# The FP4 feed-forward stage: magnitudes on ScalarE, products read from PSUM by VectorE, and the norm taken block by block

## The reference, cut to what matters

```python
def fp4_quant_dequant(x):
    xb = x.reshape(shape[:-1] + (shape[-1] // 16, 16))
    scale = jnp.maximum(jnp.max(jnp.abs(xb), axis=-1, keepdims=True) / 6.0, 1e-12)
    xn = xb / scale
    idx = jnp.searchsorted([0.25, 0.75, 1.25, 1.75, 2.5, 3.5, 5.0], jnp.abs(xn))
    return ([0.0, 0.5, 1.0, 1.5, 2.0, 3.0, 4.0, 6.0][idx] * jnp.sign(xn) * scale).reshape(shape)

def fp4_linear(x, w):
    return jnp.einsum('bsk,nk->bsn', fp4_quant_dequant(x), fp4_quant_dequant(w))

def _L2_ffn_ref(x, w_gate, w_up, w_down):            # 128 -> 352 -> 128
    h = jax.nn.silu(fp4_linear(x, w_gate)) * fp4_linear(x, w_up)
    return fp4_linear(h, w_down)

x = x + _L2_ffn_ref(_layernorm(x), w_gate, w_up, w_down)   # layernorm eps 1e-5, no gain or bias
```

## Time and profile before

| | us |
|---|---|
| median of 3 runs | 6759.97 |
| the profiled execution, its own time | 6756.28 |
| its span | 6754.2 |
| the stage of the change within the span | 5973 to 6452.7 |

### The profile page before, as it was taken

One profiled execution on the slowest core, in us unless ns is written; L12 is line 12 of the kernel. 1 busy time (PEld: TensorE's weight loads), 2 busy tenths in 40 slices (PEclk: granted clock), 3 DMA queues, 4 the chain that ended last, 5 costly groups with the idle time before them and its releaser, 6 DMA issues. The chain is left out here.

```text
span 6754.2 us, 122147 instructions
## 1 busy us (share of the span) xinstructions
PE 5795.9 (86%) x38509; PEld 3594.7 (53%) x38509; DVE 4329.9 (64%) x9722; ACT 2805.1 (42%) x4568; POOL 1939.8 (29%) x2617
## 2 busy tenths in 40 slices
PE   8996999999993998889987998799888889845567
PEld 5773444444442776467745775477545556523454
DVE  6874666666655775367736774477545466669965
ACT  4552222222221554345543554355444455412244
POOL 5440000000003553255414552355310022333312
PEclk9998999999996999899998999899988899867789
DMA  4332222233223553155504551355300000000002
GB/s 129 104 101 91 96 96 95 96 96 97 95 93 82 144 149 94 31 143 146 138 4 131 149 150 33 88 145 149 80 4 0 3 0 0 4 3 0 0 2 57
DMA packets 526309, 526.84 MB, mean 78 GB/s; under 512 B 55698, under 2 KB 436705, under 8 KB 503780
## 3 DMA queue, kind: packets, MB, share of 16 engines
q1 hardware_dynamic: 526004, 523.15, 27.6%
HBM read 337.88 MB, written 185.07 MB: 77 GB/s over the span
## 5 line engine op out<-in xcount | busy, mean ns | idle before, releaser
L362 DVE TENSOR_REDUCE a_mx<-a_unit 128x2 f32<-128x512 f32 (+1 forms) x1920 | 1294.3, 684 | 574.8 <-PE a_unit L538 562.6
L452 ACT ACTIVATE a_prob<-a_slot 128x1536 f32<-128x1536 f32 x640 | 929.0, 1452 | 740.9 <-PE a_slot L561 448.5
L536 PE MATMUL a_unit<-a_sk,a_sq 96*128 96x256 bf16 (+3 forms) x5120 | 756.3, 251 | 75.2 <-DMA a_sk<-a_kscratch 54.1
L1148 ACT ACTIVATE f_silu<-f_pG 128x512 f32<-128x512 f32 x528 | 315.1, 598 | 939.3 <-PE f_pG L1221 939.1
L1094 DVE TENSOR_TENSOR f_gated<-f_spread,f_silu 128x512 f32<-128x512 f32 x512 | 354.3, 692 | 402.8 <-ACT f_silu L1148 358.3
L538 PE MATMUL a_unit<-a_maskq,identb 128*128 128x256 bf16 (+1 forms) x1920 | 606.3, 316 | 0.0
L1200 PE MATMUL f_pO<-f_hidden,f_wd 128*128 128x512 f32 x1056 | 546.3, 599 | 17.0 <-DVE f_hidden L1096 16.3
L536 PEld LDWEIGHTS a_unit<-a_sk,a_sq 96*128 96x128 bf16 (+1 forms) x5120 | 385.3, 99 | 312.1 <-issue 124.8
L1221 PE MATMUL f_pG<-f_xnT,f_wg 128*128 128x512 f32 x1056 | 541.5, 594 | 0.0
L1225 PE MATMUL f_pU<-f_xnT,f_wu 128*128 128x512 f32 x1056 | 540.9, 594 | 0.0
L60 POOL TENSOR_SCALAR f_veps<-f_moments 128x4 f32<-128x4 f32 (+1 forms) x112 | 25.4, 227 | 1731.3 <-DVE f_moments L1002 1271.4
(11 more groups left out here) (394 smaller groups left out, 11507.0 us busy)
## 6 DMA issues: line engine op xcount, KB each, us to landing
f_spread<-f_scratch SPq DMA_DIRECT2D x1024, 128.0 KB, 2.9
a_sq<-a_qscratch SPq DMA_DIRECT2D x128, 768.0 KB, 5.7
a_sk<-a_kscratch SPq DMA_DIRECT2D x160, 384.0 KB, 6.6
a_qscratch<-a_parts SPq DMA_DIRECT2D x288, 192.0 KB, 2.2
a_qscratch<-a_parts SPq DMA_DIRECT2D x288, 128.0 KB, 2.2
a_kscratch<-a_parts SPq DMA_DIRECT2D x160, 192.0 KB, 2.2
a_kscratch<-a_parts SPq DMA_DIRECT2D x160, 128.0 KB, 2.1
a_qscratch<-a_parts SPq DMA_DIRECT2D x288, 64.0 KB, 1.8
```

The lines of the kernel that those rows point to most:

```text
L362: v.tensor_reduce(dst, src, op=ALU.max, axis=AX.X, negate=True).then_inc(red_done, 1)
L452: act.activation(prob[gr % 2][:, :], slot[:, :], ACT.Exp, scale=SCALE).then_inc(exp_done, 1)
L536: pe.matmul(bank[:, at * wide:(at + 1) * wide], q, sk[b][0:KM, gr * GH + h, 0:wide], start=(at == 0), stop=False)
L1148: act.activation(silu[c % 2][:, :], pG[c % 2][:, :], ACT.Silu).then_inc(silu_done, 1)
```

## The change

`fp4_feed_forward` is rewritten; no other stage is touched.

- `row_moments` is no longer called. VectorE takes `bn_stats` and `bn_aggr` of block n+2 in `step(n)`, GpSimd makes `rstd` and `shift = -mean * rstd` for its four tiles (four instructions of 128x4), and ScalarE writes `xn = x * rstd + shift`, one activation per tile.
- SyncE no longer waits before the loads; GpSimd zeroes only the 32 unused partitions of two slices of `raw`.
- The quantiser is in three parts. `scaled` (five instructions) gives the signed `y = x / scale`; ScalarE writes `|y| * (2^22+1)` (`absx`, `absh`); `rounded` is two scalar_tensor_tensor on the signed numbers, `y = max(mag, c) + y`, then `y = max(mag, c) - y`, which leaves the rounded number with its sign turned; `unscaled` multiplies by a scale that is kept negative.
- The copies `up` are gone. VectorE multiplies `pU` in PSUM with `silu`; `product(0)` of block m stands between `rounded` and `unscaled` of block n, products 1 to 3 behind `unscaled`. `hid` has one buffer.
- TensorE's matmuls of tile t >= 2 wait for the product of tile t-2 (`hid_done`), where they waited for its SiLU.
- All engines step from n = -2; the weights are quantised at the end of that step.

```diff
-    row_moments(nc, core, tag + "m_", core["x"], 1e-5)
...
-        centred = k.sb("centred", [P, BT, D])
+        stats = k.sb("stats", [P, BT, 6]); moments = k.sb("moments", [P, BT, 2]); mhalf = k.sb("mhalf", [P, BT])
+        veps = k.sb("veps", [P, BT]); rstd = k.sb("rstd", [P, BT]); away = k.sb("away", [P, BT]); shift = k.sb("shift", [P, BT])
         xn = k.sb("xn", [P, BT, D]); xq = k.sb("xq", [P, BT, D]); xqT = k.sb("xqT", [P, BLK])
-        amax = k.sb("amax", [P, WIDE // B16]); scl = k.sb("scl", [P, WIDE // B16]); inv = k.sb("inv", [P, WIDE // B16])
-        mag = k.sb("mag", [P, WIDE]); low = k.sb("low", [P, WIDE]); high = k.sb("high", [P, WIDE])
+        amax = k.sb("amax", [P, WIDE // B16])
+        nscx = k.sb("nscx", [P, BLK // B16]); nsch = k.sb("nsch", [P, WIDE // B16]); inv = k.sb("inv", [P, WIDE // B16])
+        yx = k.sb("yx", [P, BLK]); yh = k.sb("yh", [P, WIDE]); absx = k.sb("absx", [P, BLK]); absh = k.sb("absh", [P, WIDE])
         silu = [k.sb(f"silu{b}", [P, I]) for b in range(2)]
-        up = [k.sb(f"up{b}", [P, I]) for b in range(2)]
-        hid = [k.sb(f"hid{b}", [P, BT, I]) for b in range(2)]; hq = k.sb("hq", [P, BT, I])
+        hid = k.sb("hid", [P, BT, I]); hq = k.sb("hq", [P, BT, I])
         hT = [k.sb(f"hT{b}", [P, 3 * P]) for b in range(2)]
...
+        by16 = lambda x: x.rearrange("p (b e) -> p b e", e=B16)
...
-                sp.wait_ge(setup, 1)
...
-                g.memset(raw[:, :, :], 0.0).then_inc(setup, 1)
-
...
+                chain = Chain(g)
+                chain.link(g.memset(mhalf[:, :], -0.5))
+                for c in (2, 5):
+                    g.memset(raw[I - 2 * P:P, c, :], 0.0).then_inc(setup, 1)
+                    g.drain()
+
+                def step(i, j):
+                    n = i * 2 + j
+                    if is_block(n + 2):
+                        g.wait_ge(stats_done, n + 3)
+                        if is_block(n + 1):
+                            g.wait_ge(xn_done, n + 2)
                         g.sem_inc(apart, 1)
...
+                        chain.link(g.tensor_scalar_add(veps[:, :], moments[:, :, 1], 1e-5))
+                        g.tensor_scalar(away[:, :], moments[:, :, 0], -1.0, None, ALU.mult)
+                        chain.link(g.tensor_tensor(rstd[:, :], veps[:, :], mhalf[:, :], op=ALU.pow))
+                        g.tensor_tensor(shift[:, :], away[:, :], rstd[:, :], op=ALU.mult).then_inc(rstd_done, 1)
+                blocks_by_two(g, step)
 
...
-                def quantise(src, dst, width):
+                link = chain.link
+                def scaled(src, dst, nsc, width):
                     nb = width // B16
...
+                    link(v.tensor_reduce(amax[:, 0:nb], by16(src), op=ALU.max, axis=AX.X, apply_absolute_value=True))
+                    link(v.tensor_scalar(nsc, amax[:, 0:nb], -1.0 / 6.0, -1e-12, ALU.mult, ALU.min))
+                    link(v.tensor_scalar(inv[:, 0:nb], nsc, -HALF_DOWN, None, ALU.mult))
+                    link(v.reciprocal(inv[:, 0:nb], inv[:, 0:nb]))
+                    return v.tensor_tensor(by16(dst), by16(src), inv[:, 0:nb].unsqueeze(2).broadcast_to((P, nb, B16)),
+                                           op=ALU.mult)
+                def rounded(y, magnitude):
+                    link(v.scalar_tensor_tensor(out=y, in0=magnitude, scalar=STEP_HALF, in1=y, op0=ALU.max, op1=ALU.add))
+                    link(v.scalar_tensor_tensor(out=y, in0=magnitude, scalar=STEP_HALF, in1=y, op0=ALU.max,
+                                                op1=ALU.subtract))
+                def unscaled(dst, y, nsc, width):
+                    return v.tensor_tensor(by16(dst), by16(y), nsc.unsqueeze(2).broadcast_to((P, width // B16, B16)),
+                                           op=ALU.mult)
+                def weights():
+                    v.wait_ge(w_in, 80)
+                    v.wait_ge(setup, 2)
+                    flat = lambda x: x.rearrange("p c d -> p (c d)")
+                    link(scaled(flat(raw[:, :, :]), yh[:, 0:WGU], nsch[:, 0:WGU // B16], WGU))
+                    link(scaled(rawd[:, :], yx[:, 0:I], nscx[:, 0:I // B16], I))
+                    v.sem_inc(wy_done, 1)
+                    v.wait_ge(wa_done, 1)
+                    rounded(yh[:, 0:WGU], absh[:, 0:WGU])
+                    rounded(yx[:, 0:I], absx[:, 0:I])
+                    unscaled(flat(wdone[:, :, :]), yh[:, 0:WGU], nsch[:, 0:WGU // B16], WGU)
+                    link(unscaled(wdoned[:, :], yx[:, 0:I], nscx[:, 0:I // B16], I))
+                    v.sem_inc(wq_done, 1)
+                def step(i, j):
+                    n = i * 2 + j
+                    m = n + 1
+                    flat = lambda x: x[:, :, :].rearrange("p t d -> p (t d)")
+                    def product(t):
+                        if not is_block(m):
+                            return
+                        v.wait_ge(silu_done, m * BT + t + 1)
+                        v.tensor_tensor(hid[:, t, :], pU[t % 2][:, 0:I], silu[t % 2][:, :], op=ALU.mult).then_inc(hid_done, 1)
                     v.drain()
...
+                    if is_block(m):
+                        v.wait_ge(xn_done, m + 1)
+                        scaled(flat(xn), yx[:, :], nscx[:, :], BLK).then_inc(yx_done, 1)
+                        v.drain()
+                    if is_block(n):
+                        scaled(flat(hid), yh[:, :], nsch[:, :], WIDE).then_inc(yh_done, 1)
+                    if is_block(n + 2):
+                        src = rows(core["x"], (n + 2) * BT, BT)
+                        for t in range(BT):
+                            ins = v.bn_stats(stats[:, t, :], src[:, t, :])
+                        link(ins)
+                        for t in range(BT):
+                            ins = v.bn_aggr(moments[:, t, :], stats[:, t, :])
+                        ins.then_inc(stats_done, 1)
+                    if is_block(n - 1):
+                        dst = rows(core["x"], (n - 1) * BT, BT)
+                        v.wait_ge(o_pe, n)
                         v.tensor_tensor(dst, pO[:, :].rearrange("p (t d) -> p t d", d=D), dst, op=ALU.add
                                         ).then_inc(x_done, 1)
...
+                    if is_block(m):
+                        v.wait_ge(ax_done, m + 1)
+                        rounded(yx[:, :], absx[:, :])
+                        if is_block(n):
+                            v.wait_ge(t_pe, n + 1)
+                        unscaled(flat(xq), yx[:, :], nscx[:, :], BLK).then_inc(xq_done, 1)
+                    if is_block(n):
+                        v.wait_ge(ah_done, n + 1)
+                        rounded(yh[:, :], absh[:, :])
+                    product(0)
+                    if is_block(n):
+                        if is_block(n - 1):
                             v.wait_ge(h_pe, n * BT)
...
+                        unscaled(flat(hq), yh[:, :], nsch[:, :], WIDE).then_inc(hq_done, 1)
+                    for t in range(1, BT):
+                        product(t)
+                    if isinstance(n, int) and n == -2:
+                        weights()
+                blocks_by_two(v, step)
...
+                    def gate(t):
+                        if not is_block(m):
+                            return
+                        act.wait_ge(gu_pe, m * BT + t + 1)
+                        if t >= 2:
+                            act.wait_ge(hid_done, m * BT + t - 1)
+                        act.activation(silu[t % 2][:, :], pG[t % 2][:, 0:I], ACT.Silu).then_inc(silu_done, 1)
+                    if is_block(m):
+                        act.wait_ge(yx_done, m + 1)
+                        act.activation(absx[:, :], yx[:, :], ACT.Abs, scale=TWO_BITS).then_inc(ax_done, 1)
+                    if is_block(n):
+                        act.wait_ge(yh_done, n + 1)
+                        act.activation(absh[:, :], yh[:, :], ACT.Abs, scale=TWO_BITS).then_inc(ah_done, 1)
+                    if is_block(m):
                         act.wait_ge(t_pe, m + 1)
                         act.activation(xqT[:, :], pT[:, :], ACT.Copy).then_inc(xqT_done, 1)
+                    gate(0)
+                    gate(1)
+                    if is_block(n + 2):
+                        act.wait_ge(rstd_done, n + 3)
+                        src = rows(core["x"], (n + 2) * BT, BT)
                         for t in range(BT):
...
+                            ins = act.activation(xn[:, t, :], src[:, t, :], ACT.Identity, bias=shift[:, t:t + 1],
+                                                 scale=rstd[:, t:t + 1])
+                        ins.then_inc(xn_done, 1)
+                    gate(2)
+                    gate(3)
+                    if is_block(n):
                         for t in range(BT):
...
-                                pe.wait_ge(silu_done, m * BT + t - 1)
+                                pe.wait_ge(hid_done, m * BT + t - 1)
...
+def is_block(m):
+    return not isinstance(m, int) or 0 <= m < BLOCKS
```

(17 more changed lines are left out.)

108 lines of the change are left out of this document (23 added, 85 removed).

## The result

The changed kernel takes **6654.81 us**, the median of four runs (6647.52 to 6656.29), against 6755.81 (6746.72 to 6768.34, four runs) for the kernel before: a ratio of **0.9847**, 95% interval 0.9829 to 0.9866. Forecast were 6673 and a range of 6645 to 6703. The profiled execution is one of the four, 6656.29 us with a span of 6654.4, and its mean granted clock is 0.934 (0.928 before).

A forecast was written before the change was run, and what follows sets the result against it. VectorE's instruction list was taken to bound the blocks. Savings of 47.6 (pass), 2.4 (weights) and 36.9 (blocks), 86.9 in all, took the profiled 6756.3 to 6669.4; that execution being 3.7 below the median, 6673 us, range 6645 to 6703.

The forecast's parts named there:

- The pass: Ahead of the blocks: the pass over all rows goes, so the loads start with the stage, -47.6 us.
- The weights: Quantising the weights ahead of the blocks: fewer VectorE instructions per matrix, an added trip to ScalarE, net -2.4 us.
- The blocks: The 16 blocks: lead, fifteen periods of 22.8 and tail together 376.8 us against 413.7, -36.9.
- lead to product(0): Start of block 0: input quantised 6.4, low-clock path 5.0, table load 1.3, ScalarE's weight copies 0.5, together 13.2 us.
- VectorE's list: VectorE's instructions per block: 13.02 removed, 8.01 added, boundaries and small waits another 0.7 less; 24.97 becomes 19.3 us.
- The waits: VectorE per block: 1.6 ahead of product 0 plus 2.0 for products 2 and 3, less 0.1 overlap; none for the addition.
- the clock stays high: Rival, TensorE in the blocks: no fall to 1.2 GHz, period 20.9, 32 us less, 6641; chance 0.12.
- My value of 1.5 for the norms: ScalarE's four norms ahead of the third SiLU delay VectorE's products by between 0 and 4 x 0.46; 1.5 taken.
- Clock low throughout: Rival, TensorE in the blocks: clock stays low, period 24.7, tail 5 longer, 34 us more, 6707; chance 0.14.
- Table reloads: Rival, ScalarE in the blocks: three table loads on the path per block, 62 us more, 6735; chance 0.03.
- GpSimd's small instructions: Rival, in the blocks: four per block hold the port shared with VectorE and delay roundings, 32 us more, 6705; chance 0.04.
- The ring through the addition: Rival, in the blocks: the chain from hq through addition and xq to the next hq sets the period, 6775; chance 0.02.

The follow-up runs named there:

- pass_back: The changed kernel with the pass over all rows (row_moments) called again ahead of the stage, its results unused: 6704.85 us.
- warm56: The changed kernel with 56 transposes of the identity on TensorE ahead of its wait for xq in every block, results overwritten: ratio 0.9813.
- norm_first: The changed kernel with ScalarE's four norms moved ahead of gate(0) instead of between gate(1) and gate(2): ratio 0.9838.
- gps_products: The changed kernel with the four products hid given back to GpSimd, with ScalarE's copies up: ratio 0.9824.
- gps_norm: gps_products with ScalarE's four norms moved ahead of gate(0): ratio 0.9829.
- gps_norm_warm24: gps_norm with 24 transposes of the identity on TensorE ahead of its wait for xq: ratio 0.9794.

## Why the prediction was right, point by point

**The pass** (forecast -47.6): the loads start 0.0 us behind the stage's start; with pass_back the term measures 47.9. **The weights** (forecast -2.4): from first load to the first block 15.9 us, 18.2 before: -2.3.

**The blocks** (forecast -36.9) measure 360.7 against 413.7, -53.0, and here all of the error lies:

| | forecast | measured |
|---|---|---|
| lead to product(0) | 13.2 | 11.3 (5991.45 to 6002.74) |
| 15 distances, product(0) to product(0) | 338.6 | 324.9 (to 6327.66) |
| a distance between additions | 22.8 | 21.85 |
| VectorE's list in it | 19.3 | 18.26 |
| waits in it | 3.5 | 3.59 |
| tail | 25 | 24.5 |

**The mis-sized term is VectorE's list.** The window of one block of the kernel before, against the one of 22.42 us above:

```profile
6107.94:6132.91 24.97, 13.45 (x58) 10.36 (x58) 22.61 (x25) 6.04 (x17) 7.61 (x4) 0.73 0.00 0
```

VectorE's busy time fell from 22.6 to 17.0 us, 5.6, where the forecast had 5.0; and what lay between its instructions besides the waits above fell from 2.4 to 1.35, 1.0 where the forecast had 0.7. Three things make the difference of 1.0, read over the first twelve blocks of both profiles:

- Overlap, 0.35. An instruction that is not linked by a drain starts before the recorded end of the one ahead of it: `bn_stats` at 6101.51, 0.09 before the end of L1841. The change has five or six such boundaries a block, 0.06 to 0.09 us each, 0.43 in all; the kernel before has one, of 0.08. The forecast priced these instructions at their full durations.
- Drained boundaries, 0.3. The forecast counted five fewer. Counted in the code they go from 24 to 15 a block, nine fewer, at 0.07 to 0.08 us each.
- Prices, 0.26. The forecast took the instructions that go from the earlier trace rows (2.12 and 1.42), which are means that include the last block, without GpSimd's products. In the blocks of the loop they last 2.19 and 1.46.

The rest is that the mean distance before is 24.91 and not the 24.97 of the one block that the forecast started from. With the 0.1 that the waits were longer, fifteen distances are 13.7 us shorter than forecast, of 16.1 in all.

**The lead** was 1.9 too long: I set the table load (1.3) and the copies of the weights (0.5) on the path, and neither is. The load lies beside TensorE's first tile; the copies (5993.48 to 5994.8) only delay the magnitude, which ends at 5995.30, while VectorE is busy with the next statistics until 5995.27.

**The waits** were the uncertain part of the list and came out right: 1.6 forecast and 1.87 measured ahead of product 0, 2.0 and 1.72 for the others, 0 for the addition and for the magnitudes. So was the clock: 1.2 GHz for the first tiles after an idle stretch of 7.1 us (forecast 7.3), back at 2.4 before tile 3. warm56 shows the cause: with the clock held up, the distance falls by 1.9, as much as the rival case "the clock stays high" was given (22.8 to 20.9). My value of 1.5 for the norms, between 0 and 1.8, was wrong: norm_first shows that they cost 0, since TensorE's matmuls end as late. By the forecast's own figure (8 us less for norms at 0, 0.5 a block) its 2.0 would have been 1.5; that 2.0 lies as near to the measured 1.72 is partly luck.

**The rivals.** Clock low throughout: no, it rises in tile 2. Table reloads: one load in the stage. The Trainium skill's "ScalarE: Activation LUTs", "Table sets: the hidden batching unit", has copy, identity and abs in every set; the trace agrees, since SiLU, copy, identity and abs alternate behind a single load. GpSimd's small instructions: L1824 takes 0.67 beside L1846 where it took 0.23 alone, but VectorE's L1847 beside them takes 0.72 instead of 0.69. So the lock is there, and costs 0.03. The ring through the addition: no wait on `q_pO` before the tail.

**What the forecast didn't ask** is whether each part was worth its place. It booked four products at 0.53 as a cost and left it at that; gps_products shows that without them the stage is 16.5 us shorter. No run put back the old rounding or the normalisation on VectorE; what those two parts gained is read from the durations and not from an experiment.

## What to carry to other kernels

Price a list of instructions by start-to-start distances, drained and undrained apart and both counted in the code, and take each duration from a row in which the port's other user is as it will be: an instruction of 1.42 beside GpSimd's products was one of 0.89 without them. Where an engine waits for TensorE behind an idle stretch, look at the granted clock before reordering anything: at 1.2 GHz three reorderings moved the waits about and gained 0 to 3 us, while filler transposes took 25 us off.

## What was not expected of the hardware

- In these traces GpSimd and VectorE take turns by whole instructions: a product of 0.93 becomes 2.10 when it starts beside a rounding of 1.62, and the next rounding becomes 2.20. A 128x32 instruction of 0.18 can take 0.79 in that way.
- The time at which the clock rises isn't set by the block's own work alone: gps_products and gps_norm do the same work per block, with idle stretches of 5.8 and 4.9 us ahead of `xq`, and have 0.83 and 0.75. In gps_norm_warm24, with equal work in each block, the last distances go 17.8, 18.8, 20.0, 18.5, 17.8, 18.8. What sets this pattern stays open.
- An instruction of VectorE that isn't held by a drain starts 0.06 to 0.09 us before the recorded end of the one ahead; with a drain it starts 0.07 to 0.08 us behind it.
- Transposes of 128x128 in float32 follow one another every 0.112 us at 2.4 GHz (56 in 6.28).
